# Adding expert results to the output by an accumulating indirect scatter

## The reference, cut to what matters

```
x = x + ga * attention(layernorm(x) * (1 + ca) + sa)
h = layernorm(x) * (1 + cb) + sb
score = softmax(h @ Wg + bg); gate = max(score); idx = argmax(score)
pos = place of the token among those of its expert; keep = pos < 512
buf[idx, pos] = h                                  # kept tokens only
y = relu(buf @ W1 + b1) @ W2 + b2                  # per expert
x = x + gb * where(keep, y[idx, pos] * gate, 0)
```

## Time and profile before

| | us |
|---|---|
| median of 3 runs | 1819.06 (1818.73 to 1821.21) |
| the profiled execution | 1820.85 |
| its span, first to last instruction | 1819.3 |
| TensorE busy | 1786.2 (98%) |
| VectorE busy | 1115.3 (61%) |
| ScalarE busy | 894.3 (49%) |
| GpSimd busy | 612.2 (34%) |
| the chain that ended last | 90% TensorE, 2% ScalarE, 1% VectorE |
| mean granted TensorE clock | 0.992 of full |

### The profile page before, as it was taken

The page is one execution under the profiler, slowest core; times in us unless marked ns, Lnnn a source line. Parts: engine busy times, 40 slices in busy tenths (PEclk is TensorE's granted clock), DMA queues, the critical chain, the costliest instruction groups (busy, mean ns, idle before and its releaser), DMA issues.

```text
span 1819.3 us, 27932 instructions
## 1 busy us (share of the span) xinstructions
PE 1786.2 (98%) x9151; PEld 1496.6 (82%) x9152; DVE 1115.3 (61%) x1963; ACT 894.3 (49%) x1317; POOL 612.2 (34%) x564
## 2 busy tenths in 40 slices
PE   9999999999999799999999999998998999999998
PEld 5788888888888588899888888888888888888886
DVE  6577887887887554446445444457558675444753
ACT  4446546546546344345444444347467664434741
POOL 1145555555554422023030303043235431304303
PEclk9999999999999899999999999999999999999999
DMA  7586767767777454354443524265446553426522
GB/s 266 192 229 186 201 154 200 194 163 196 189 192 220 91 162 159 108 183 150 159 163 112 174 98 162 98 199 200 159 143 224 195 207 134 155 98 204 205 81 78
DMA packets 148429, 304.09 MB, mean 167 GB/s; under 512 B 18097, under 2 KB 18493, under 8 KB 146326
## 3 DMA queue, kind: packets, MB, share of 16 engines
q1 hardware_dynamic: 115098, 221.01, 35.3%
q0 software_dynamic: 33280, 82.42, 19.0%
HBM read 254.29 MB, written 67.43 MB: 177 GB/s over the span
## 4 chain that ended last, share of the span: by engine, by line
PE 90%; ACT 2%; DVE 1%; issue 1%; ACTq 0%; POOLq 0%; DVEq 0%
PE bank L344 27%; PE bank L346 27%; PE bank L345 27%; PE bank L778 3%; PE bank L954 1%; PE bank L867 1%; PE bank L649 1%; PE bank L770 1%; PE bank L785 1%; ACT h_f L1296 1%; PE bank L748 0%; PE bank L753 0%; ACT h_hi L1295 0%; ACT w_hi L1280 0%; DVE w_lo L1735 0%
## 5 line engine op out<-in xcount | busy, mean ns | idle before, releaser
L1295 ACT ACTIVATE h_hi<-bank,b_col 128x512 fp32r<-128x512 f32 x256 | 177.0, 691 | 528.3 <-PE bank L346 486.6
L1762 DVE TENSOR_TENSOR h_lo<-h_f,h_hi 128x512 fp32r<-128x512 f32 x256 | 174.0, 690 | 350.2 <-ACT h_f L1296 280.2
L344 PE MATMUL bank<-bt_hi,w_hi 128*128 128x512 f32 (+4 forms) x1024 | 359.1, 351 | 3.7 <-DVE w_lo L1735 3.5
L345 PE MATMUL bank<-bt_lo,w_hi 128*128 128x512 f32 (+4 forms) x1024 | 358.1, 350 | 0.0
L346 PE MATMUL bank<-bt_hi,w_lo 128*128 128x512 f32 (+4 forms) x1024 | 358.1, 350 | 0.0
L344 PE MATMUL bank<-w_hi,h_hi 128*128 128x512 f32 x832 | 326.3, 392 | 2.1 <-issue 2.1
L345 PE MATMUL bank<-w_lo,h_hi 128*128 128x512 f32 x832 | 324.4, 390 | 0.0
L346 PE MATMUL bank<-w_hi,h_lo 128*128 128x512 f32 x832 | 324.2, 390 | 0.0
L2058 POOL DMA_INDIRECT out_dram<-yo,tok_x x64 | 75.5, 1180 | 672.3 <-DVE yo L1797 637.6
L344 PEld LDWEIGHTS bank<-bt_hi,w_hi 128*128 128x128 f32 x1024 | 193.2, 189 | 28.2 <-issue 5.8
L345 PEld LDWEIGHTS bank<-bt_lo,w_hi 128*128 128x128 f32 x1024 | 193.2, 189 | 21.3 <-issue 0.2
(11 more groups left out here) (309 smaller groups left out, 2952.8 us busy)
## 6 DMA issues: line engine op xcount, KB each, us to landing
raw<-in_L_ffn_W_dram SPq DMA_DIRECT2D x128, 1024.0 KB
xa<-in_L_attn_x_dram SPq DMA_DIRECT2D x16, 1024.0 KB, 8.3
xr<-in_L_attn_x_dram SPq DMA_DIRECT2D x16, 1024.0 KB, 6.7
xr<-global_rows POOLq DMA_DIRECT2D x16, 1024.0 KB, 8.8
h_rows<-sb_tab SPq DMA_DIRECT2D x16, 1024.0 KB
out_dram<-xr SPq DMA_DIRECT2D x16, 1024.0 KB, 10.0
h_rows<-h POOLq DMA_DIRECT2D x15, 1024.0 KB
b_bc<-in_L_ffn_b_dram SPq DMA_DIRECT2D x16, 256.0 KB, 6.3
```

The source lines that it names most:

```text
L344: pe.matmul(o, a_hi, b_hi, start=start, stop=False)
L345: pe.matmul(o, a_hi, b_lo, start=False, stop=False)
L1295: act.activation(h1_hi[b % 2][:, j, :], h_bank[j][:, :], ACT.Relu, bias=bias)
L1762: dve.tensor_tensor(h1_lo[b % 2][:, j, :], h1_f[:, j, :], h1_hi[b % 2][:, j, :].bitcast(F32), ALU.subtract) \
```

## The change

For the experts 0 to 14 the gated results are no longer added to gathered rows on VectorE. The scatter itself adds them to the rows in DRAM (`compute_op=ALU.add`), behind `y_scaled` of block 1, so the gather of `xo` and the function `add_results` are gone. The last expert gathers `xo` and adds on VectorE as it did.

```diff
--- before.py
+++ after.py
@@ -1789,19 +1789,12 @@
                 dve.scalar_tensor_tensor(out=yo[:, j, :], in0=yo[:, j, :], scalar=gate_x[:, j:j + 1],
                                          in1=gb_rows[:, j, :], op0=ALU.mult, op1=ALU.mult).then_inc(y_scaled, 1)
 
-        def add_results(e):
-            dve.wait_ge(xo_in, 16 * GS * (e + 1))
-            for i in range(GS):
-                q, j = 4 * e + i, GS - 1 - i
-                dve.wait_ge(y_scaled, q + 1)
-                dve.tensor_tensor(yo[:, j, :], yo[:, j, :], xo[:, j, :], ALU.add).then_inc(y_ready, 1)
-
         def last_rows(e):
 
             dve.wait_ge(b2_in, 16 * (e + 1))
             dve.wait_ge(gate_ready, e + 1)
             dve.wait_ge(gb_in, 16 * GS * (e + 1))
-            dve.wait_ge(xo_in, 16 * GS * (e + 1))
+            dve.wait_ge(xo_in, 16 * GS)
             for j in range(GS):
                 dve.wait_ge(y_sent[j], 16 * e)
                 dve.scalar_tensor_tensor(out=yo[:, j, :], in0=b2_bc[:], scalar=gate_x[:, j:j + 1],
@@ -1871,8 +1864,7 @@
                     gate_results(e - 1)
                 if b == 2:
                     if not first:
-                        add_results(e - 1)
-                        dve.wait_ge(y_ready, 4 * e)
+                        dve.wait_ge(y_scaled, 4 * e)
                         stand_alone(dve, dve_passed)
 
                     dve.tensor_copy(tok_x[par][:], tok[:, bass.ds(GS * e, GS), 0]).then_inc(tok_x_ready, 1)
@@ -2047,17 +2039,25 @@
             pool.wait_ge(tok_x_ready, 2 * e + 2)
             stand_alone(pool, pool_passed)
             gather(gb_rows, mod_dram.rearrange("b r d -> (b r) d"), tok_g, gb_in, NBATCH * 7)
-            gather(xo, out_rows, tok_x[par], xo_in)
+            if isinstance(e, int) and e == E - 1:
+                gather(xo, out_rows, tok_x[par], xo_in)
 
         def finish_rows(e, par):
 
             for i in range(GS):
                 q, j = 4 * e + i, GS - 1 - i
-                pool.wait_ge(y_ready, q + 1)
-                stand_alone(pool, pool_passed)
-                pool.indirect_dma_start(out=out_rows, out_offset=bass.IndirectOffsetOnAxis(tok_x[par][:, j:j + 1], 0),
-                                        in_=yo[:, j, :], in_offset=None, bounds_check=T - 1, oob_is_err=False) \
-                    .then_inc(y_sent[j], 16)
+                target = bass.IndirectOffsetOnAxis(tok_x[par][:, j:j + 1], 0)
+                if isinstance(e, int) and e == E - 1:
+
+                    pool.wait_ge(y_ready, i + 1)
+                    pool.indirect_dma_start(out=out_rows, out_offset=target, in_=yo[:, j, :], in_offset=None,
+                                            bounds_check=T - 1, oob_is_err=False).then_inc(y_sent[j], 16)
+                else:
+                    pool.wait_ge(y_scaled, q + 1)
+                    stand_alone(pool, pool_passed)
+                    pool.indirect_dma_start(out=out_rows, out_offset=target, in_=yo[:, j, :], in_offset=None,
+                                            bounds_check=T - 1, oob_is_err=False, compute_op=ALU.add) \
+                        .then_inc(y_sent[j], 16)
 
         for par in range(2):
             pool.wait_ge(x2_stored[par], 16 * (NG // 2))
```

## The result

The changed kernel took 1824.86 us (median of 12 runs, 1823.48 to 1825.45), the kernel before 1819.64 us (12 runs, 1818.59 to 1821.93). The ratio is 1.0026, 95% interval 1.0019 to 1.0034: slower by 0.26%, where 1825.0 us was predicted. The profiled execution took 1824.68 us with a span of 1822.8 us.

What follows compares the result with a forecast made beforehand. TensorE, busy for 98% of the span, was taken to bound the kernel. W1's lateness in two experts, 2 x 3.3 - 0.7 = 5.9 us, added to the median 1819.06 gave 1825.0 us (+0.32%), range 1821.5 to 1828.5.

Steps and rivals of the forecast that it cites:

- The place and the chain: In two experts with few rows, early scatters delay the next expert's W1, then relus 1 to 3, transposes and TensorE.
- Work removed counts 0: 60 additions on VectorE (41.0 us) and 60 gathers on GpSimd (80 us) are off the path, so removing them gives 0.
- D: Rival, chance 0.06: VectorE's removed additions were what it is late with in the two experts; 5.5 us faster, 1813.6 us.
- Accumulation at 7.1 us per MB, even alternation: Accumulating packets cost 7.1 us per MB and alternate one to one with the load's, leaving it 0.13 MB per us.
- So this load arrived 0.4 us ahead of its use in the one and 0.3 us ahead in the other: Slack of the next expert's W1 in the two experts, read from its last bytes; 0.7 us taken off the sum.
- 3.8 to 4.9 us before the first packet: Delay from the end of GpSimd's instruction to the transfer's first packets, taken from two places in the trace before.
- The start of GpSimd's first instruction: First gating ends at about 1241.0, the instruction takes 1.8 us, so it ends at about 1242.9.
- The four scatters follow each other by 1.8 + 0.3 us with 0.26 MB each: GpSimd issues an expert's four accumulating scatters closely enough to keep the alternation with W1's load going.
- The term of 3.3 us per expert: W1's lateness in each of the two experts, the middle of 4.3 and 2.3 us; bounds 0 and 7.4.
- For a longer pause I add nothing on the clock: Longer waits of TensorE in the two experts were given no added time for its clock.
- B: Rival, chance 0.15: accumulation shares the DMA engines from the end of GpSimd's first instruction; +11.7 us, 1830.8 us.
- C: Rival, chance 0.29: loads requested first finish first and the accumulation fills the time behind them; no change, 1819.1 us.

Runs made afterwards that it cites:

- gating late: Changed kernel with gate_results moved from block 1 to block 2, where the additions stood, the scatters following it: 1822.59 us, ratio 1.0012.

## Why the prediction was right, step by step

- **The place and the chain.** Right. W1 late at L1285, relus late, transposes at L954 late, in the two sparse experts and no others. The request moved ahead takes the loss away.
- **Work removed counts 0.** Right for the time in this order: the waits behind w_lo are unchanged and D is out. The 80 us less on GpSimd were 42, mainly since each scatter takes longer. It is not a property of the additions: with gating moved next to them they cost 7.9 us.
- **Accumulation at 7.1 us per MB, even alternation.** The alternation is right: in 1248 to 1249 the queues moved 61 and 75 packets. The price is too high beside a load: 28.3% of 5 us for 0.26 MB is 5.4 us per MB, and so was the store of the earlier trace rows, 70.6% of 5 us for 0.66 MB. With plain packets in the same place W1 is late by 0.67 and 0.25 us and not by 1.51 and 0.97.
- **"So this load arrived 0.4 us ahead of its use in the one and 0.3 us ahead in the other".** Wrong. The reading takes the last bytes for the arrival. From request to use it was 8.3 and 8.4 us, and in "gating late", where ScalarE waited for the same load, 8.2 and 8.4. So the load was 0 us ahead, and the 0.7 us that the sum takes off were not there.
- **3.8 to 4.9 us before the first packet.** Right: 4.3 and 4.4 us.
- **The start of GpSimd's first instruction.** This was mis-sized, and it is most of the error in the first stretch. The prediction lets the scatter start when the first gating ends, at 1241.0. It starts 0.9 us after that end (1240.58, then 1241.49), as in the kernel before the scatter of the earlier trace rows, at 1251.33, did behind the first addition of the earlier trace rows, which ends at 1250.4. So the first packet came 6.4 us after the request of W1, where the middle of the prediction's two cases is 5.5. By the prediction's own working that leaves 0.40 MB of the earlier trace rows, which take 3.1 us in place of 1.5: 1.6 us late. Measured were 9.9 us from request to use in place of 8.3, of which ScalarE waited 1.51. In the second stretch the same start leaves 0.45 MB and gives 1.9 us; it was 1.0, where the first scatter had only 0.09 MB.
- **"The four scatters follow each other by 1.8 + 0.3 us with 0.26 MB each".** Wrong: the second was held for 7.1 us, most likely by VectorE's row of two-input operations, and the first of the second stretch had 0.09 MB. In the first stretch it changes little. With 1.9 us on GpSimd and 4.3 us to its first packet, a second scatter would have begun at about 1250, when less than 1 us of the load was left; that is an estimate from these rows, and no run has four scatters that are not held.
- **The term of 3.3 us per expert** thus measured 1.5 and 1.0, and the 5.9 us at L954 became 2.6.
- **"For a longer pause I add nothing on the clock".** This was wrong by 0.8 us: behind the second wait the granted clock was 0.50 for 6.8 us in place of 3.4, and the stretch grew by 3.4 us where the waits grew by 2.6.
- **The last expert as before, 0.** Its code moved too; the ending took 0.7 us longer and the time outside the span 0.3. Missed.
- **The sum.** The forecast of +5.9 us against +5.2 in the medians and +3.8 in the traces. That it was so near is in part luck, from errors that cancel: 3.3 us too much at W1 and 0.5 us that the other experts gave back, against 0.8 us of clock and 1.0 us of ending left out, and 1.4 us by which the profiled executions differ from the medians.
- **B and C.** Out. B has packets of the scatter from the end of GpSimd's instruction, and the first came 4.3 and 4.4 us later. C has no wait for W1, and it is there, 1.5 and 1.0 us. But with W1 requested first, and so less load ahead of it, the first packet came only 1.8 and 1.6 us after the instruction: the 3.8 to 4.9 us are no fixed time.

## What to carry to other kernels

Work that is hidden can still move a transfer: when a change releases a DMA earlier, look for the load with the least room in that stretch, count how many of the new transfers can really be under way in it (the engine that issues them may be held), and give the load room by asking for it first. A removed operation is worth what the order around it makes it worth: nothing here where it stood behind a wait, 8 us where the same work had been gathered into one block. And when a wait shrinks, ask whether it was the time that a load needed.

## What the runs showed of the hardware

- An indirect scatter with accumulation takes GpSimd 1.55 us where nothing disturbs it, the plain one 0.97.
- The same scatter of 128 rows (0.26 MB) beside a weight load took 1.4 us of the 16 DMA engines with accumulation and 0.65 plain.
- Behind 2.25 MB of requested loads a scatter moved its first packet 4.3 and 4.4 us after GpSimd's instruction had ended; with W1 requested first it was 1.8 and 1.6 us.
- A scatter issued beside a back-to-back row of two-input operations of VectorE was held for 7.1 us, to the row's end, accumulating or plain, in two stretches, and took 1.57 us when it was issued behind the row. Beside similar rows in other runs scatters took 1.2 to 1.9 us, so the row alone does not decide it.
- Waits of TensorE between 2.9 and 4.6 us were followed by 0, 3.4 or 6.8 us at a granted clock of 0.50, and not in the order of their length.
- GpSimd's last instruction and the time outside the span differ between kernels whose last scatters are the same: 5.85, 6.20, 6.51 and once 8.38 us, and 1.5 to 1.9 us.
